# Ternary layers: a slot's last token tile between the third and the fourth product, in three slots its first one ahead of the sixth

## The chip, the cores and the metric

The kernel runs on one core of a Trainium2 chip. Its five engines run their own instruction streams and meet at semaphores: TensorE (PE; its weight loads are shown apart as PEld), VectorE (DVE), ScalarE (ACT), GpSimd (POOL) and SyncE (SP, which here issues all transfers). The metric is the time of one execution on the device in microseconds; the kernel before took 1720.47 us (median of 3 runs, 1720.34 to 1723.22).

## The reference, cut to what matters

2048 tokens of width 512 (4 x 512 tokens; every half-step works on 1024 tokens at once) go through six blocks. The change touches the two ternary feed-forward blocks alone.

```python
x = x + 0.5 * _L0_ffn_ref(_layernorm(x), W1, W2, W3)      # hidden width 2048, Hadamard transform
x = x + _L0_attn_ref(_layernorm(x), qkv, o_proj, ...)     # causal attention
x = x + 0.5 * _L0_ffn_ref(_layernorm(x), W1, W2, W3)
x = x + 0.5 * _L1_ffn_ref(_layernorm(x), gate_w, up_w, down_w, gate_s, up_s, down_s)   # ternary
x = x + _L1_attn_ref(_layernorm(x), B, C, D)              # state = tanh(x B'); state C' + D x
x = x + 0.5 * _L1_ffn_ref(_layernorm(x), gate_w, up_w, down_w, gate_s, up_s, down_s)   # ternary

def _L1_ffn_ref(x, gate_w, up_w, down_w, gate_s, up_s, down_s):   # weights are -1, 0 or 1; width 1408
    g = jnp.einsum('th,ih->ti', xf, gate_w) * gate_s
    u = jnp.einsum('th,ih->ti', xf, up_w) * up_s
    hdn = jax.nn.silu(g) * u
    out = jnp.einsum('ti,hi->th', hdn, down_w) * down_s
```

## The kernel before, in words

**Passes and slots.** A feed-forward block on 1024 tokens (a pair of 512-token chunks) is a pass. There are eight: numbers 0 to 3 are of kind "A" (hidden width 2048), and 4 to 7 of kind "B", the ternary ones, two before and two after the small state-space block. A ternary pass has 11 slots, 0 to 10. A slot computes one block of 128 hidden units, gate and up, for both chunks, and TensorE works the slots off one after the other in `run`.

**The seven products.** Gate and up times two chunks would be eight products of this size; the kernel forms seven from sums of operands. They are run as p1, p5, p6, p2 (`first_half`) and p7, p3, p4 (`second_half`). A product is 2 contraction blocks, and each of these 2 matmuls of 128x512 in a ternary pass, where the weights have no low part (4 matmuls in all): the values are split in a high and a low part, which are multiplied apart (L521, L523, L525 in `three`). Results lie in banks BX, BY, BZ, BW, BV of PSUM (0 to 4). Between the products other engines move partial sums: ScalarE copies BX to BY after p1 (`seed_y`, L1270), for which p6 waits; it copies BY to BW after p7 (`seed_w`, L1319), for which p4 waits; VectorE adds BY and the kept p5 into BZ after p6 (`seed_z`, L1956), for which p7 waits. Then come VectorE's sum L1960, its two products with the gate (`gated`, L1967 behind ScalarE's L1328, and L1971 behind p4), and the split of the hidden block in high (ScalarE, L1291) and low (VectorE, `hid_low`, L1946).

**Token tiles.** The down projection of a group of 2 or 3 finished hidden blocks is done in tiles of 128 tokens by 512 outputs, 4 matmuls (6 for the group of 3). A pass has 8 tiles for each group, four of them, here called t0 to t3, in each of the slots 3 to 9. They stand between p2 and p7. TensorE writes a tile to a bank, and VectorE adds it to y (`add_tile`, L1926 for the first group, L1929 for others). Slots 0, 1, 2 and 10 have no tiles.

**Transposes.** The next pass needs its input, normed and transposed. In four slots of each of passes 4, 5 and 6 (4 to 7, in pass 5 5 to 8), TensorE transposes two normed tiles, n0 and n1, 4 matmuls of 128x128 each (`turn_tiles`, L763), between t3 and p7; ScalarE copies them out (L1155). Pass 7 has none. In pass 5 GpSimd also multiplies these normed tiles by a row and adds them to x (L1736, L1737).

**What sets the order and the banks.** The order of instructions on each engine is written out by hand. The banks of tiles and transposes are dealt out beforehand in `Plan`: 5, 6, 7 in turn, in the order t0, t1, t2, t3, n0, n1. Before a tile or a transpose is written, `bank_free` waits for the reader of the bank's user before it: for n0 that is the add of t1, and for n1 the add of t2. On VectorE the add of t0 stands ahead of `seed_z` (`behind` in `ternary_slot`), and the other three behind it, with statistics and final adds of the pass before between them in some slots (`extra`).

**Weights.** SyncE issues the loads in order: for each slot the up and gate weights of the next one (`w13_load`, 1.8 MB in three transfers, after p4 of the slot before) and a w2 block of 512 KB (`w2_load`, L565) in one of four places, after the last tile of the group that used the place. The first group, of blocks 0 to 2, ends with slot 4's t3; block 4 goes in block 0's place, and slot 5's tiles need it.

Of the kernel before, what the change touches and what calls it, by code (L numbers as in the profile page):

```python
# [74 lines left out]
class Pass:  # L75
# [4 lines left out]
    def __init__(self, no, kind, li, pair, u0, v0, w2_0):  # L80
        self.no, self.kind, self.li, self.pair = no, kind, li, pair
        self.u0, self.v0, self.n, self.w2_0 = u0, v0, UNITS[kind], w2_0
        self.groups = GROUPS[kind]
        self.offset = 2 if no == 0 else 0

        self.open = (1, 2, self.n - 1) if kind == "B" else ()
        self.norms = NORMS.get(no, tuple(range(self.offset + 3, self.offset + 3 + PT // 2)))
        self.turn_slots = TURNS.get(no, tuple(range(self.offset + 4, self.offset + 4 + PT // 2)))
        self.downs = [[] for _ in range(self.n + 1)]
        self.turns = [[] for _ in range(self.n + 1)]  # L90
# [111 lines left out]
def build(nc, t):  # L202
# [8 lines left out]
    with ExitStack() as ctx:  # L211
# [510 lines left out]
        def _(pe):  # L722
# [58 lines left out]

            def first_half(ps, s, exact):
                u, v = ps.u0 + s, ps.v0 + s
# [28 lines left out]
                if after_ternary(ps, s):  # L812
                    pe.wait_ge(added, ended_before(ps, END_BANKS.index(BV)))
                product(ps, s, "p5", BV, True, exact, p5_done)
                pe.wait_ge(y_seeded, u + 1)
                product(ps, s, "p6", BY, False, exact, p6_done)
                product(ps, s, "p2", BX, False, exact, p2_done)

            def second_half(ps, s, exact):
                u = ps.u0 + s  # L820
                pe.wait_ge(z_seeded, u + 1)
                product(ps, s, "p7", BY, False, exact, p7_done)
                product(ps, s, "p3", BZ, False, exact, p3_done)
                pe.wait_ge(w_seeded, u + 1)
                product(ps, s, "p4", BW, False, exact, p4_done)
# [51 lines left out]
            def run(ps, exact=False):  # L877
                early = ps.no == BEFORE_T - 1
                for s in range(ps.n):
                    first_half(ps, s, exact)  # L880
                    if s == ps.n - 1:
# [4 lines left out]
                    if ps.no == BEFORE_T and s == 2:  # L886
                        pe.wait_ge(att_added, CH * TT)
                    for k, (g, i, d) in enumerate(ps.downs[s]):
                        down(ps, g, i, d, exact)
                        if early and k == 0 and s < ps.n - 1:  # L890
                            turn_tiles(ps, s)
                    if s < ps.n - 1:
                        if not early:
                            turn_tiles(ps, s)
                        second_half(ps, s, exact)
                if ps.kind == "B":
# [892 lines left out]
        def _(dve):  # L1789
# [80 lines left out]
            def sums(ps, step):  # L1870
# [10 lines left out]
                elif step == 2:  # L1881
                    dve.wait_ge(sums_ready, 4 * ps.no + 2)
                    tt(xn[:, 0:2, :], b22, t2, ALU.subtract).then_inc(sums_ready, 1)
                else:
                    tt(xn[:, 2:4, :], b21, t2, ALU.subtract).then_inc(sums_ready, 1)

# [74 lines left out]

            def gated(ps, s):
                u = ps.u0 + s
# [3 lines left out]
                nc.vector.scalar_tensor_tensor(own(u), own(u), scale, other(u), ALU.mult,  # L1967
                                               ALU.mult).then_inc(c22_read, 1)
                dve.wait_ge(c11_read, u + 1)
                dve.wait_ge(p4_done, ps.v0 + s + 1)  # L1970
# [148 lines left out]
            def ternary_slot(ps, s):  # L2119
# [19 lines left out]
                for k, (g, i, d) in enumerate(ps.downs[s]):  # L2139
                    if k or not behind:  # L2140
                        add_tile(ps, g, i, d)
# [3 lines left out]
                sum_c22(u)  # L2145
                gated(ps, s)
                if follower(ps) and s in END_SUMS:
# [328 lines left out]
```

## Time and profile before

| | |
|---|---|
| median of 3 runs | 1720.47 us (1720.34 to 1723.22) |
| profiled execution, own time | 1721.68 us |
| its span | 1719.9 us |
| PE busy | 1702.7 us, 99% |
| VectorE, ScalarE busy | 67%, 48% |
| granted TensorE clock | full in all 40 slices of the span |
| the four ternary passes with the state-space block | from 1201.25 to the end at 1719.9 us |

The profile is of one execution, and its times count from the start of its span. A matmul is shown with 0.39 us, but it overlaps the next one: what counts is the distance from one start to the next. A weight load (PEld) runs ahead of its matmul, so an idle time in front of a load need not be one of the matmuls. "[0.19 <-ACT psum L1319]" behind a row says that the engine idled 0.19 us before it and what ended that.

### The profile page before, as it was taken

The page shows a single profiled execution, that of the slowest core. Times are in us where ns is not written, and L with a number is a line of the kernel's source. Part 1 is how long each engine was busy: PE and PEld are TensorE (multiplying, and loading weights), DVE is VectorE, ACT ScalarE, POOL GpSimd, SP SyncE. Part 2 cuts the span into 40 slices and gives each one's busy share as a digit, 9 for nine tenths or more (in the row PEclk, how much of TensorE's full clock was granted, in tenths as well). Part 3 has the DMA queues.
Part 4 walks back from the last instruction along what each step waited for, and adds up shares of the span by engine and source line. Part 5 has one row for each costly group of instructions (what it writes and reads, how often), then busy time and mean ns, then how long its engine had stood idle before and what let it go on. Part 6 is the DMA issues. An engine that isn't in the chain of part 4 may idle for free.

```text
span 1719.9 us, 21451 instructions
## 1 busy us (share of the span) xinstructions
PE 1702.7 (99%) x7696; PEld 1391.1 (81%) x7696; DVE 1154.5 (67%) x1806; ACT 824.3 (48%) x1350; POOL 124.9 (7%) x184
## 2 busy tenths in 40 slices
PE   7999999999999999999999999999999999999998
PEld 5788888888888888888888888888787778787786
DVE  8977678677775555754446554457668769867866
ACT  5745544455675543434223343223556456655534
POOL 1000000000012220000000000000000144100001
PEclk9999999999999999999999999999999999999999
DMA  9775555699985000244345343344656653466666
GB/s 331 266 287 216 220 198 194 237 364 367 371 337 206 1 1 1 106 170 151 137 154 193 137 165 137 148 156 165 220 220 223 237 211 118 146 221 227 233 220 221
DMA packets 89627, 340.34 MB, mean 198 GB/s; under 512 B 9392, under 2 KB 20016, under 8 KB 83888
## 3 DMA queue, kind: packets, MB, share of 16 engines
q1 hardware_dynamic: 89520, 338.94, 53.1%
q8 instruction: 64, 1.05, 0.3%
q14 instruction: 43, 0.35, 0.1%
HBM read 259.73 MB, written 79.17 MB: 197 GB/s over the span
## 4 chain that ended last, share of the span: by engine, by line
PE 93%; DVE 4%; issue 1%; ACT 1%; DMA 1%; POOL 0%; SPq 0%; ACTq 0%; DVEq 0%
PE psum L521 34%; PE psum L523 29%; PE psum L525 26%; PE psum L763 2%; DVE xc_lo L1889 1%; DVE x L1922 1%; PE psum L732 0%; DMA w<-w_kept 0%; DVE att_lo L1863 0%; PE psum L1000 0%; DVE hid L1946 0%; DMA x<-in_w2a 0%; DVE w L1909 0%; ACT fw_hi L1128 0%; DVE psum L1956 0%
## 5 line engine op out<-in xcount | busy, mean ns | idle before, releaser
L521 PE MATMUL psum<-xc_hi,w 128*128 128x512 f32 x1544 | 609.9, 395 | 2.1 <-DVE xc_lo L1889 1.0
L523 PE MATMUL psum<-xc_lo,w 128*128 128x512 f32 x1544 | 602.3, 390 | 0.0
L525 PE MATMUL psum<-xc_hi,w 128*128 128x512 f32 x928 | 361.3, 389 | 0.0
L521 PEld LDWEIGHTS psum<-xc_hi,w 128*128 128x128 f32 x1544 | 289.8, 188 | 84.0 <-ACT psum L1270 8.1
L521 PE MATMUL psum<-w,hid 128*128 128x512 f32 x864 | 338.0, 391 | 0.6 <-DVE y L1929 0.2
L525 PE MATMUL psum<-w,hid 128*128 128x512 f32 x864 | 336.5, 390 | 0.0
L523 PEld LDWEIGHTS psum<-xc_lo,w 128*128 128x128 f32 x1544 | 290.1, 188 | 56.7
L1922 DVE TENSOR_TENSOR x<-psum,x 128x512 f32<-128x512 f32 x256 | 173.2, 688 | 149.1 <-PE psum L525 148.8
L523 PE MATMUL psum<-w,hid 128*128 128x512 f32 x544 | 211.8, 389 | 0.0
L1946 DVE TENSOR_TENSOR hid<-sg,hid 128x512 fp32r<-128x512 f32 x216 | 148.9, 699 | 93.4 <-ACT hid L1291 91.4
L525 PEld LDWEIGHTS psum<-xc_hi,w 128*128 128x128 f32 x928 | 174.2, 188 | 36.4
L521 PEld LDWEIGHTS psum<-w,hid 128*128 128x128 f32 x864 | 162.1, 188 | 39.5 <-DVE x L1922 4.5
L525 PEld LDWEIGHTS psum<-w,hid 128*128 128x128 f32 x864 | 162.2, 188 | 33.8
L1319 ACT ACTIVATE psum<-psum 128x512 f32<-128x512 f32 x108 | 62.9, 582 | 232.2 <-PE psum L525 174.3
L1291 ACT ACTIVATE hid<-sg 128x512 fp32r<-128x512 f32 x208 | 127.8, 627 | 75.6 <-DVE sg L1967 55.1
L1960 DVE TENSOR_TENSOR sg<-psum,sg 128x512 f32<-128x512 f32 x108 | 74.4, 689 | 87.9 <-ACT psum L1319 86.7
L1270 ACT ACTIVATE psum<-psum 128x512 f32<-128x512 f32 x108 | 62.9, 582 | 120.0 <-PE psum L523 58.3
L523 PEld LDWEIGHTS psum<-w,hid 128*128 128x128 f32 x544 | 102.2, 188 | 20.5
L1956 DVE TENSOR_TENSOR psum<-psum,sg 128x512 f32<-128x512 f32 x108 | 75.0, 694 | 43.5 <-PE psum L525 36.8
L1707 POOL TENSOR_SCALAR var_eps<-meanvar 128x4 f32<-128x4 f32 x24 | 6.6, 275 | 1266.7 <-DVE meanvar L1809 875.7
L1313 ACT ACTIVATE sg<-psum 128x512 f32<-128x512 f32 x64 | 38.0, 593 | 89.2 <-PE psum L525 89.2
L1150 ACT ACTIVATE xn<-x,shift,rstd 128x512 f32<-128x512 f32 x88 | 65.8, 808 | 14.1 <-POOL shift L1710 14.1
(164 smaller groups left out, 2010.0 us busy)
## 6 DMA issues: line engine op xcount, KB each, us to landing
w<-w_kept SPq DMA_DIRECT2D x186, 448.0 KB, 4.3
w<-w_kept SPq DMA_DIRECT2D x93, 896.0 KB, 6.4
w<-w_kept SPq DMA_DIRECT2D x94, 512.0 KB, 7.2
w_kept<-w SPq DMA_DIRECT2D x16, 1792.0 KB, 7.4
w_kept<-prep SPq DMA_DIRECT2D x12, 1792.0 KB, 7.6
w_kept<-w SPq DMA_DIRECT2D x16, 512.0 KB, 6.3
w_kept<-prep SPq DMA_DIRECT2D x12, 512.0 KB, 8.9
att_raw<-in_att_w SPq DMA_DIRECT2D x4, 1024.0 KB, 9.0
```

The source lines that it names most:

```text
L521: pe.matmul(out, a_hi, b_hi, start=start, stop=False, skip_group_check=onto)
L523: last = pe.matmul(out, a_hi, b_lo, start=False, stop=stop and zero == "a", skip_group_check=onto)
L525: last = pe.matmul(out, a_lo, b_hi, start=False, stop=stop, skip_group_check=onto)
L1150: return copy(out, x[:, i, :], AF.Identity, bias=shift[:, i:i + 1], scale=rstd[:, i:i + 1])
L1270: copy(bank(BY), bank(BX), AF.Copy).then_inc(y_seeded, 1)
L1291: copy(hid_of(u, c)[:, 0, :], own(u) if c else sg[:, 0, :], AF.Copy).then_inc(hid_hi_ready, 1)
L1313: copy(sg[:, 0, :], bank(BX), AF.Silu, scale=gate_scale(ps, s)).then_inc(c11_read, 1)
L1319: copy(bank(BW), bank(BY), AF.Copy).then_inc(w_seeded, 1)
L1922: tt(at_x, b, at_x, ALU.add).then_inc(added, 1)
L1946: tt(h[:, 1, :], source, h[:, 0, :], ALU.subtract).then_inc(hid_ready, 1)
L1956: tt(bank(BZ), bank(BY), own(u), ALU.add).then_inc(z_seeded, 1)
L1960: tt(own(u), bank(BY), own(u), ALU.add).then_inc(c22_ready, 1)
```

## The change

In a ternary pass `run` takes the last tile, t3, out of the slot's list and hands it to `second_half`, which puts it between p3 and p4. In slots 4, 6 and 8 (`ps.ahead`) it takes t0 out too and hands it to `first_half`, which puts it between p5 and p6. In slots with transposes these now stand directly behind t2. On VectorE, t3's add goes from ahead of the sum L1960 into `gated`, between L1967 and L1971. One sum of VectorE, step 3 of `sums`, gets a wait on the sum of step 1, since an add that stood between is gone. `Plan`, and with it every bank, is as before.

```diff
--- before.py
+++ after.py
@@ -84,6 +84,8 @@
         self.offset = 2 if no == 0 else 0
 
         self.open = (1, 2, self.n - 1) if kind == "B" else ()
+
+        self.ahead = [s for blocks in self.groups[:-1] for s in (blocks[-1] + 2,) if kind == "B" and s < self.n - 1]
         self.norms = NORMS.get(no, tuple(range(self.offset + 3, self.offset + 3 + PT // 2)))
         self.turn_slots = TURNS.get(no, tuple(range(self.offset + 4, self.offset + 4 + PT // 2)))
         self.downs = [[] for _ in range(self.n + 1)]
@@ -779,7 +781,7 @@
                                  xc_lo[:, X_OF[name], k, :], start and k == 0, k == 1, "a" if exact else None, not start)
                 last.then_inc(done, 1)
 
-            def first_half(ps, s, exact):
+            def first_half(ps, s, exact, ahead=()):
                 u, v = ps.u0 + s, ps.v0 + s
                 if ps.no == 0:
                     pe.wait_ge(w13_ready, s + 1)
@@ -812,15 +814,19 @@
                 if after_ternary(ps, s):
                     pe.wait_ge(added, ended_before(ps, END_BANKS.index(BV)))
                 product(ps, s, "p5", BV, True, exact, p5_done)
+                for tile in ahead:
+                    down(ps, *tile, exact)
                 pe.wait_ge(y_seeded, u + 1)
                 product(ps, s, "p6", BY, False, exact, p6_done)
                 product(ps, s, "p2", BX, False, exact, p2_done)
 
-            def second_half(ps, s, exact):
+            def second_half(ps, s, exact, between=()):
                 u = ps.u0 + s
                 pe.wait_ge(z_seeded, u + 1)
                 product(ps, s, "p7", BY, False, exact, p7_done)
                 product(ps, s, "p3", BZ, False, exact, p3_done)
+                for tile in between:
+                    down(ps, *tile, exact)
                 pe.wait_ge(w_seeded, u + 1)
                 product(ps, s, "p4", BW, False, exact, p4_done)
 
@@ -877,7 +883,12 @@
             def run(ps, exact=False):
                 early = ps.no == BEFORE_T - 1
                 for s in range(ps.n):
-                    first_half(ps, s, exact)
+                    tiles, ahead, between = ps.downs[s], (), ()
+                    if ps.kind == "B" and tiles:
+                        tiles, between = tiles[:-1], tiles[-1:]
+                    if s in ps.ahead:
+                        tiles, ahead = tiles[1:], tiles[:1]
+                    first_half(ps, s, exact, ahead)
                     if s == ps.n - 1:
                         second_half(ps, s, exact)
                         turn_tiles(ps, s)
@@ -885,14 +896,14 @@
                         pe.wait_ge(fw_out, 16)
                     if ps.no == BEFORE_T and s == 2:
                         pe.wait_ge(att_added, CH * TT)
-                    for k, (g, i, d) in enumerate(ps.downs[s]):
+                    for k, (g, i, d) in enumerate(tiles):
                         down(ps, g, i, d, exact)
                         if early and k == 0 and s < ps.n - 1:
                             turn_tiles(ps, s)
                     if s < ps.n - 1:
                         if not early:
                             turn_tiles(ps, s)
-                        second_half(ps, s, exact)
+                        second_half(ps, s, exact, between)
                 if ps.kind == "B":
                     fill(ps, exact)
                 for g, i, d in ps.downs[ps.n]:
@@ -1882,6 +1893,7 @@
                     dve.wait_ge(sums_ready, 4 * ps.no + 2)
                     tt(xn[:, 0:2, :], b22, t2, ALU.subtract).then_inc(sums_ready, 1)
                 else:
+                    dve.wait_ge(sums_ready, 4 * ps.no + 2)
                     tt(xn[:, 2:4, :], b21, t2, ALU.subtract).then_inc(sums_ready, 1)
 
             def convert(ps, m):
@@ -1959,13 +1971,15 @@
                 dve.wait_ge(w_seeded, u + 1)
                 tt(own(u), bank(BY), own(u), ALU.add).then_inc(c22_ready, 1)
 
-            def gated(ps, s):
+            def gated(ps, s, tile=None):
                 u = ps.u0 + s
                 scale = up_s[:, s:s + 1] if ps.kind == "B" else 1.0
                 dve.wait_ge(c12_read, u + 1)
                 dve.wait_ge(c22_ready, u + 1)
                 nc.vector.scalar_tensor_tensor(own(u), own(u), scale, other(u), ALU.mult,
                                                ALU.mult).then_inc(c22_read, 1)
+                if tile:
+                    add_tile(ps, *tile)
                 dve.wait_ge(c11_read, u + 1)
                 dve.wait_ge(p4_done, ps.v0 + s + 1)
                 nc.vector.scalar_tensor_tensor(sg[:, 0, :], bank(BW), scale, sg[:, 0, :], ALU.mult,
@@ -2137,13 +2151,13 @@
                 elif not ps.downs[s]:
                     extra(ps, s, 1)
                 for k, (g, i, d) in enumerate(ps.downs[s]):
-                    if k or not behind:
+                    if 0 < k < len(ps.downs[s]) - 1:
                         add_tile(ps, g, i, d)
                     extra(ps, s, k + 1)
                 if follower(ps) and s in LAST_SUMS:
                     sums(follower(ps), LAST_SUMS[s])
                 sum_c22(u)
-                gated(ps, s)
+                gated(ps, s, ps.downs[s][-1] if behind else None)
                 if follower(ps) and s in END_SUMS:
                     sums(follower(ps), END_SUMS[s])
                 if last:
```

In the three places below the changed kernel's lines have other numbers: L523, L525, L527, L765 are L521, L523, L525, L763 of before, and on VectorE L1941, L1958, L1968, L1972, L1979, L1985 are L1929, L1946, L1956, L1960, L1967, L1971. First TensorE in slot 5 of pass 4, around the transposes (xn). Rows with w_54,hid are tiles, rows with xc_hi or xc_lo are products. Before: the last two matmuls of t2, t3, the transposes, and the start of p7:

```order
L521 MATMUL psum<-w_54,hid 128x512
L525 MATMUL psum<-w_54,hid 128x512
L521 MATMUL psum<-w_54,hid 128x512 [waits added]
L525 MATMUL psum<-w_54,hid 128x512
L521 MATMUL psum<-w_54,hid 128x512
L525 MATMUL psum<-w_54,hid 128x512
L763 MATMUL psum<-ident,xn 128x128 [waits xn_ready,added]
L763 MATMUL psum<-ident,xn 128x128 x3
L763 MATMUL psum<-ident,xn 128x128 [waits xn_ready,added]
L763 MATMUL psum<-ident,xn 128x128 x3
L521 MATMUL psum<-xc_hi,w_53 128x512 [waits z_seeded]
```

After, from the third matmul of t2:

```order
L523 MATMUL psum<-w_54,hid 128x512
L527 MATMUL psum<-w_54,hid 128x512
L765 MATMUL psum<-ident,xn 128x128 [waits xn_ready,added]
L765 MATMUL psum<-ident,xn 128x128 x3
L765 MATMUL psum<-ident,xn 128x128 [waits xn_ready,added]
L765 MATMUL psum<-ident,xn 128x128 x3
L523 MATMUL psum<-xc_hi,w_53 128x512 [waits z_seeded]
```

t3 is gone from its place, and the transposes follow t2.

The same slot from the end of p3 to the start of the next slot's p1 (which waits for c11_read). Before:

```order
L521 MATMUL psum<-xc_hi,w_53 128x512
L523 MATMUL psum<-xc_lo,w_53 128x512
L521 MATMUL psum<-xc_hi,w_53 128x512 [waits w_seeded]
L523 MATMUL psum<-xc_lo,w_53 128x512
L521 MATMUL psum<-xc_hi,w_53 128x512
L523 MATMUL psum<-xc_lo,w_53 128x512
L521 MATMUL psum<-xc_hi,w_53 128x512 [waits c11_read,w13_in0]
```

After:

```order
L523 MATMUL psum<-xc_hi,w_53 128x512
L525 MATMUL psum<-xc_lo,w_53 128x512
L523 MATMUL psum<-w_54,hid 128x512 [waits added]
L527 MATMUL psum<-w_54,hid 128x512
L523 MATMUL psum<-w_54,hid 128x512
L527 MATMUL psum<-w_54,hid 128x512
L523 MATMUL psum<-xc_hi,w_53 128x512 [waits w_seeded]
L525 MATMUL psum<-xc_lo,w_53 128x512
L523 MATMUL psum<-xc_hi,w_53 128x512
L525 MATMUL psum<-xc_lo,w_53 128x512
L523 MATMUL psum<-xc_hi,w_53 128x512 [waits c11_read,w13_in0]
```

t3, with its wait for a free bank, stands between p3 and p4, which waits for w_seeded.

VectorE in a slot of pass 4 with tiles and without statistics (y is a tile's add, psum the seed of BZ, the first sg the sum, the next two `gated`, hid the low parts). Before:

```order
L1929 TENSOR_TENSOR y<-psum,y 128x512 [waits added,down_ready]
L1956 TENSOR_TENSOR psum<-psum,sg 128x512 [waits c12_read,p5_kept,p6_done]
L1929 TENSOR_TENSOR y<-psum,y 128x512 [waits added,down_ready] x3
L1960 TENSOR_TENSOR sg<-psum,sg 128x512 [waits w_seeded]
L1967 SCALAR_TENSOR_TENSOR sg<-sg,small 128x512 [waits c22_ready,c12_read]
L1971 SCALAR_TENSOR_TENSOR sg<-psum,small,sg 128x512 [waits p4_done,c11_read]
L1946 TENSOR_TENSOR hid<-sg,hid 128x512 [waits hid_hi_ready] x2
```

After:

```order
L1941 TENSOR_TENSOR y<-psum,y 128x512 [waits added,down_ready]
L1968 TENSOR_TENSOR psum<-psum,sg 128x512 [waits c12_read,p5_kept,p6_done]
L1941 TENSOR_TENSOR y<-psum,y 128x512 [waits added,down_ready] x2
L1972 TENSOR_TENSOR sg<-psum,sg 128x512 [waits w_seeded]
L1979 SCALAR_TENSOR_TENSOR sg<-sg,small 128x512 [waits c22_ready,c12_read]
L1941 TENSOR_TENSOR y<-psum,y 128x512 [waits added,down_ready]
L1985 SCALAR_TENSOR_TENSOR sg<-psum,small,sg 128x512 [waits p4_done,c11_read]
L1958 TENSOR_TENSOR hid<-sg,hid 128x512 [waits hid_hi_ready] x2
```

One of the three adds behind the seed went between the two rows of `gated`.

## Rows read from the trace of the kernel before

**Rows 1.** The page's first lines: busy time of each engine.
```profile
span 1719.9 us, 21451 instructions
...
PE 1702.7 (99%) x7696; PEld 1391.1 (81%) x7696; DVE 1154.5 (67%) x1806; ACT 824.3 (48%) x1350; POOL 124.9 (7%) x184
```

**Rows 2.** Waits, 1201 us to the end: in total, times, longest.
```profile
PEld psum L521 <- ACT psum L1270: 8.1, 44, 0.2
PEld psum L521 <- ACT psum L1319: 8.1, 43, 0.2
...
PEld psum L521 <- DVE psum L1956: 5.6, 16, 0.8
```

**Rows 3.** Timeline (start, length), TensorE, pass 7: starts of t0, p7, p4, p6, next t0.
```profile
1659.69 0.39 PE L521 MATMUL psum<-w,hid 128*128 128x512 f32 x1
...
1663.31 0.39 PE L521 MATMUL psum<-xc_hi,w 128*128 128x512 f32 x1
...
1665.13 0.43 PE L521 MATMUL psum<-xc_hi,w 128*128 128x512 f32 x1
...
1667.93 0.42 PE L521 MATMUL psum<-xc_hi,w 128*128 128x512 f32 x1
...
1669.79 0.39 PE L521 MATMUL psum<-w,hid 128*128 128x512 f32 x1
```

**Rows 4.** Timeline, the same slot: ScalarE's copy for p4, and p4's weight load.
```profile
1664.42 0.58 ACT L1319 ACTIVATE psum<-psum 128x512 f32<-128x512 f32 x1 [3.84 <-PE psum L523]
...
1665.05 0.19 PEld L521 LDWEIGHTS psum<-xc_hi,w 128*128 128x128 f32 x1 [0.19 <-ACT psum L1319]
```

**Rows 5.** Timeline, TensorE, pass 4 slot 5: t0, t2's last, transposes, p7.
```profile
1249.89 0.39 PE L521 MATMUL psum<-w,hid 128*128 128x512 f32 x1
...
1252.38 0.39 PE L525 MATMUL psum<-w,hid 128*128 128x512 f32 x1
...
1253.52 1.04 PE L763 MATMUL psum<-ident,xn 128*128 128x128 f32 x8
1254.31 0.47 PE L521 MATMUL psum<-xc_hi,w 128*128 128x512 f32 x1
```

**Rows 6.** Timeline, VectorE, the same slot.
```profile
1250.99 0.69 DVE L1929 TENSOR_TENSOR y<-psum,y 128x512 f32<-128x512 f32 x1 [1.24 <-PE psum L525]
1251.60 0.69 DVE L1956 TENSOR_TENSOR psum<-psum,sg 128x512 f32<-128x512 f32 x1
1252.20 1.30 DVE L1929 TENSOR_TENSOR y<-psum,y 128x512 f32<-128x512 f32 x2
```

**Rows 7.** Timeline, pass 5 slot 6: three adds, and the transposes' loads.
```profile
1379.80 1.87 DVE L1929 TENSOR_TENSOR y<-psum,y 128x512 f32<-128x512 f32 x3
...
1380.53 0.42 PEld L763 LDWEIGHTS psum<-ident,xn 128*128 128x128 f32 x4 [0.43 <-DVE y L1929]
1381.13 0.42 PEld L763 LDWEIGHTS psum<-ident,xn 128*128 128x128 f32 x4 [0.17 <-DVE y L1929]
...
1381.54 0.47 PE L521 MATMUL psum<-xc_hi,w 128*128 128x512 f32 x1
```

**Rows 8.** Timeline, pass 5 slots 5 and 6: t2's add, p7, VectorE's low parts.
```profile
1368.52 0.67 DVE L1929 TENSOR_TENSOR y<-psum,y 128x512 f32<-128x512 f32 x1
...
1369.66 0.47 PE L521 MATMUL psum<-xc_hi,w 128*128 128x512 f32 x1
...
1375.38 3.31 DVE L1946 TENSOR_TENSOR hid<-sg,hid 128x512 fp32r<-128x512 f32 x2 [0.70 <-ACT hid L1291]
```

**Rows 9.** Timeline, ScalarE, pass 4 slots 9 and 10: last seed, then L1270.
```profile
1299.21 0.59 ACT L1421 ACTIVATE psum<-y 128x512 f32<-128x512 f32 x1
1300.50 0.58 ACT L1270 ACTIVATE psum<-psum 128x512 f32<-128x512 f32 x1 [0.70 <-PE psum L523]
```

**Rows 10.** The w2 load of pass 4 slot 4, its landing, and the page's median.
```profile
1242.72 0.32 SPq L565 DMA_DIRECT2D w<-w_kept  x1
...
DMA to landing us min/median/max: 3.1/3.1/3.1
...
w<-w_kept SPq DMA_DIRECT2D x94, 512.0 KB, 7.2
```

## Prediction

> **What bounds the kernel now.** I read the page's busy line first, then the waits, then the timeline of single slots. TensorE is busy 1702.7 of 1719.9 us [rows 1], so only an idle stretch of TensorE, or work added to it, can move the time. The table of waits shows how little idle time the ternary passes have left: 43 weight loads waited 8.1 us in total for ScalarE's copy at L1319 (the copy that seeds bank BW for the fourth product, p4), and 44 waited 8.1 us for its copy at L1270 (which seeds BY for the sixth, p6); for VectorE's seeding of BZ (L1956) 16 waited 5.6 us [rows 2]. These are waits of the weight load, which runs ahead of its matmul, so they overstate the loss. The loss is read from starts of matmuls. In one slot of the last pass 16 matmuls of tiles take 1663.31 - 1659.69 = 3.62 us, that is 0.2266 us each and no loss. Then p7 and p3, 8 matmuls, take 1665.13 - 1663.31 = 1.82 us: none lost. p4, p1 and p5, 12 matmuls, take 1667.93 - 1665.13 = 2.80 us where 12 x 0.2266 is 2.72: 0.08 us is lost, all of it behind p4's wait. p6 and p2, 8 matmuls, take 1669.79 - 1667.93 = 1.86 us against 1.81: 0.05 us behind p6's wait [rows 3]. The copy for p4 lasts from 1664.42 for 0.58 us, and p4's weight load goes at 1665.05 after 0.19 us of idling [rows 4]; had it come 0.2 us earlier, nothing would be lost.
>
> **What the change removes.** 28 slots (slots 3 to 9 of four passes) get a tile between p3 and p4: at least 4 matmuls, 0.91 us, more cover for a copy that is some 0.15 us late. That wait goes: 28 x 0.08 = 2.2 us at most. 12 slots (4, 6, 8 of four passes) get a tile ahead of p6, which removes p6's wait: 12 x 0.05 = 0.6 us at most. Neither adds or removes a matmul. So the gain cannot be over 2.8 us, and it is nothing at the low end, if the loss comes back at the next wait.
>
> **What it adds: the transposes lose their cover.** A slot's tiles and transposes share banks 5 to 7 in turn, in an order fixed before: t0, t1, t2, t3, then transposes n0 and n1. So n0 needs the bank of t1, and n1 the bank of t2, read out by VectorE. The plan isn't changed, but t3 no longer stands between t2 and n0. Take slot 5 of the first ternary pass. Tiles start at 1249.89, t2's last matmul at 1252.38, the transposes at 1253.52, p7 at 1254.31, 0.79 us after them [rows 5]. VectorE starts t0's add at 1250.99, which is 0.42 us after the start of t0's last matmul (1249.89 + 3 x 0.227 = 1250.57), then seeds BZ at 1251.60, then makes the adds of t1 and t2 from 1252.20 to 1253.50 [rows 6]. t2's add cannot be earlier: 1252.38 + 0.42 = 1252.80 is its start. Today that end, 1253.50, comes before n1 wants it. After the change n0 could start at 1252.38 + 0.23 = 1252.61 and p7 at 1253.40. But n1 waits for 1253.50, and p7 stands 0.41 us behind it. The rows for such a wait exist, in slot 6 of the second ternary pass, where the adds are late today: three adds at steps of 0.60 us end at 1380.48, 1381.07 and 1381.67, the transposes' loads go at 1380.53 (0.43 us of idling) and 1381.13 (0.17 us), 0.05 us behind the first two ends [rows 7]. p7 there starts at 1381.54. So here n1 goes at 1253.55 and p7 at 1253.96: 0.55 us later than without a wait. The same holds in slots whose t0 stands ahead of p6, since n1's bank is t2's there too, and for tiles of 6 matmuls, since only the last matmul counts.
>
> There are 12 slots with transposes (four each in the first three ternary passes). Ten are as above: 10 x 0.55 = 5.5 us. The other two are slots 5 and 6 of the second ternary pass. In slot 5 VectorE has statistics between the adds: t2's add runs 1368.52 to 1369.19 and p7 starts at 1369.66 already now [rows 8]. It starts no earlier after the change, but 0.91 us of t3 still has to follow: +0.9 us. In slot 6 VectorE is held up by its pair of L1946, 3.31 us from 1375.38, beside GpSimd's work, and n1 goes at 1381.13 in either order, since slot 5's transposes, which start GpSimd's work, stay where they are. What slot 5 lost is taken back by waits that slot 6 has now, and slot 6's own t3 follows late: 0.9 us for both together, and one p4 gain and one p6 gain (0.13 us) are swallowed.
>
> **The other moves.** VectorE does one add less before its sum L1960 and one more between its two products L1967 and L1971; it idles in each slot, and t3's add starts before p4 is done, so L1971 comes no later against TensorE: nothing, with 28 x 0.05 us on either side as a bound. BZ's seed ends at 1251.60 + 0.69 = 1252.29 and p7's load, in a slot without transposes, would be wanted at about 1252.38: just in time, 0, with at most 0.1 us in each of the 6 such slots of 4-matmul tiles. In slot 9 ScalarE's last seed of a tile (1299.21) now waits for t3's add, which stands one add behind L1967 instead of ahead of it, so that it comes about 0.7 us later (an estimate, one add of 0.69 us [rows 6]), and ends beside slot 10's L1270 (1300.50) [rows 9]: 4 x 0.05 = 0.2 us, between 0 and 0.4. The wait added to VectorE's fourth sum is on a sum two steps back: 0.
>
> The last move is a transfer. The w2 block that the next group needs first is loaded into the place freed by slot 4's last tile. Its issue is at 1242.72 and it lands 3.1 us later; slot 5 wants it at 1249.89 [rows 10, 5], 7.2 us after the issue. After the change t3 ends two products (and the transposes) later: from issue to slot 5's first load there remain p4, p1, p5, p6, p2, 5 x 0.907 = 4.5 us, less 0.2 because t3's result comes that much after p4's start (0.42 - 0.23), and less 0.2 because a weight load goes ahead of its matmul: 4.1 us. 3.1 fits in 4.1. The 1.8 MB of the next up weights are issued 0.9 us behind it; behind such loads the same transfer takes 7.2 us (median [rows 10]), ahead of them I take 3.1. The Trainium skill's page "DMA: Bandwidth & Descriptors", section on queues, rings and completion order, says that each DMA engine takes one ring's descriptors in order, which speaks for the same; no row here has the two in this order.
>
> **Sum.** +5.5 + 0.9 + 0.2 - 27 x 0.08 (2.2) - 11 x 0.05 (0.5) = +3.9 us. The profiled execution took 1721.68 us, so its like would take 1725.6; it lies 1.2 us over the median of the three runs (1720.47), from which the forecast is 1724.4. A difference that this kernel's measurement tells from none is 0.2%, 3.4 us.
>
> A rule that speaks against the gain: what the row shows is p4's load at 1665.05, held 0.19 us, and matmuls 0.08 us behind afterwards [rows 3, 4]. The page "TensorE: Matmul & The Clock Gate" of the Trainium skill (section on the array's 16 sub-arrays, queue depths) says that TensorE can pull weight loads ahead of matmuls in flight. By that rule p4's load could have gone early and its wait be free, and the removal would bring nothing; the row disagrees for a load that itself waits. The time by the rule alone is that of the first rival below.
>
> **Rivals.**
> - Gains that don't come back: the 0.08 and 0.05 us are the price of any semaphore that the load meets, and are paid at the tile's or p1's wait instead. For it: part of the 0.08 is spread over p1 and p5, which also wait. Against: the tiles have waits too, and 16 of them run at 0.2266 us. Then +6.6 us, 1727.1. Chance 0.09.
> - The w2 load comes late: shared with the up weights it takes up to 7.2 us, 3.1 more than the 4.1 there are, in four slots: 3.9 + 12.4 = 16.3 us, 1736.8; from 4.1 us landing it begins to cost. Chance 0.06.
> - The transposes wait less than I say, about half, because VectorE's adds run closer behind: +1.1 us, 1721.6. Against: 1380.53 and 1381.13 sit right behind the adds' ends. Chance 0.10.
> - The other side: the transposes don't wait at all (n1 finds t2's bank read before 1253.0), and the gains stand alone: -2.6 us, 1717.9. It decides at an add that ends within 0.6 us of the start of t2's last matmul; it takes 1.1. Chance 0.06.
>
> **Chances.** The forecast holds 0.69, with 1723.4 to 1725.5 as its own range (gain terms from 0.05 to 0.08 us a slot, waits of 0.5 to 0.6 us); 0.75 of it lies above the 3.4 us. Slower: 0.52 + 0.09 + 0.06 = 0.67. No change: 0.17 + 0.10 = 0.27. Faster: 0.06. The range goes to 1721.5 below, which is the third rival, and 1727.8 above, which holds the first; the far ends of the w2 case and the gain alone are left out.
>
> **What would show it.** In the changed profile: L1319's weight-load waits down from 43 to about 15, L1270's from 44 to about 32; new waits of transposes (PEld, L765) for VectorE's adds of y, about 12 of 0.4 to 0.5 us; p7 some 0.41 us behind the second group of transposes; no wait for w2 at slot 5's first tile. It is wrong if the transposes start 0.23 us behind t2's last matmul and run through, or if slots without transposes (the whole last pass) are not some 0.1 us shorter each.

## The result, and the profile after

The change made the kernel slower: 1725.22 us (median of 9 runs, 1724.27 to 1726.53) against 1720.47 us (9 runs, 1719.78 to 1723.22). The ratio is 1.0026, 95% interval 1.0017 to 1.0034, that is 4.75 us and between 2.9 and 5.8 us. The profiled execution took 1724.76 us with a span of 1723.0 us, 3.1 us more than that of before. The runs of before came out at 1720.47 us here, at 1720.79 us beside e1 to e4 and at 1721.42 us beside e5 to e8; every difference of medians below is taken against the one beside it.

Single executions differ by a microsecond in places that the change doesn't touch. The matmuls' starts do better: from the first tile of slot 3 to the first tile behind slot 10's products, in each ternary pass, lies all that the change moves. From the timelines, one profile of each kernel, in us (two profiles of the kernel before, its own and e5's, differ by 0.43 in the sum):

| kernel | pass 4 | pass 5 | pass 6 | pass 7 | sum | against before | median against before |
|---|---|---|---|---|---|---|---|
| before | 80.97 | 82.06 | 80.89 | 77.27 | 321.19 | | |
| the change | 82.50 | 83.46 | 82.45 | 76.58 | 324.99 | +3.80 | +4.75 |
| e1, t0 ahead only | 80.63 | 81.86 | 80.64 | 76.89 | 320.02 | -1.17 | 0.0 |
| e2, t3 between only | 82.83 | 83.78 | 82.85 | 76.93 | 326.39 | +5.20 | +4.7 |
| e3, t3 not with transposes | 80.48 | 81.73 | 80.43 | 76.60 | 319.24 | -1.95 | -1.2 |
| e4, banks in issue order | 80.24 | 80.22 | 80.24 | 76.60 | 317.30 | -3.89 | -3.1 |
| e5, before again | 80.90 | 82.02 | 80.74 | 77.10 | 320.76 | -0.43 | |
| e6, before, banks shifted | 83.00 | 84.22 | 83.09 | 77.07 | 327.38 | +6.19 | +6.4 |
| e7, w2 behind up weights | 89.94 | 91.24 | 89.68 | 83.72 | 354.58 | +33.4 | +33.7 |
| e8, transposes behind p7 | 80.33 | 80.66 | 80.35 | 76.73 | 318.07 | -3.12 | -3.6 |

Pass 7, which has no transposes, got 0.69 us shorter; the other three, with four pairs each, got 1.4 to 1.6 us longer. The waits of the changed kernel from 1201 us on, to be set against [rows 2] (engine, what waited, for what: us in total, times, longest; L1281 is L1270 of before, L1330 is L1319, L765 is L763, L1938 and L1941 are L1926 and L1929):

```profile
PEld psum L765 <- DVE y L1941: 8.9, 20, 1.0
PEld psum L523 <- ACT psum L1281: 6.1, 32, 0.2
PEld psum L523 <- DVE psum L1968: 5.6, 16, 0.8
PE psum L765 <- DVE y L1941: 2.9, 11, 0.6
PEld psum L523 <- ACT psum L1330: 2.8, 15, 0.2
PEld psum L765 <- DVE y L1938: 1.2, 2, 0.6
```

Both removed waits are gone as often as they should be: 43 became 15, a difference of 28, and 44 became 32, a difference of 12. In their place stand 22 waits of transposes for VectorE's adds, 10.1 us of weight loads, where before had 3 with 0.9 us. One of them, in slot 5 of pass 4, on TensorE, on the weight loads and on VectorE, answers to [rows 5, 6]:

```profile
1253.04 0.39 PE L527 MATMUL psum<-w,hid 128*128 128x512 f32 x1
1253.59 1.27 PE L765 MATMUL psum<-ident,xn 128*128 128x128 f32 x8 [0.17 <-DVE y L1941]
1254.62 0.47 PE L523 MATMUL psum<-xc_hi,w 128*128 128x512 f32 x1
```

```profile
1253.59 0.42 PEld L765 LDWEIGHTS psum<-ident,xn 128*128 128x128 f32 x4 [0.59 <-DVE y L1941]
1254.21 0.42 PEld L765 LDWEIGHTS psum<-ident,xn 128*128 128x128 f32 x4 [0.20 <-DVE y L1941]
```

```profile
1251.65 0.69 DVE L1941 TENSOR_TENSOR y<-psum,y 128x512 f32<-128x512 f32 x1 [1.23 <-PE psum L527]
1252.26 0.69 DVE L1968 TENSOR_TENSOR psum<-psum,sg 128x512 f32<-128x512 f32 x1
1252.86 1.30 DVE L1941 TENSOR_TENSOR y<-psum,y 128x512 f32<-128x512 f32 x2
```

t2's last matmul starts at 1253.04. The adds of t1 and t2 run from 1252.86 to 1254.16; n1's load goes at 1254.21, 0.05 us behind the second, and p7 0.41 us later. From the last matmul ahead of the transposes to p7 are 1.58 us; before they were 1.02 (1254.31 less 1253.29, the start before 1253.52 by one matmul): 0.56 us lost. n0's load waits too, for t1's add, but that is not an additional loss: n1 goes when t2 is read, whether n0 was early or late.

What the change gains is seen in pass 7. TensorE in slots 7 and 8 (the starts of p7, t3, p4, then slot 8's t0, p6, t1), against [rows 3]:

```profile
1676.38 0.39 PE L523 MATMUL psum<-xc_hi,w 128*128 128x512 f32 x1
...
1678.20 0.39 PE L523 MATMUL psum<-w,hid 128*128 128x512 f32 x1
...
1679.10 0.39 PE L523 MATMUL psum<-xc_hi,w 128*128 128x512 f32 x1
...
1681.82 0.39 PE L523 MATMUL psum<-w,hid 128*128 128x512 f32 x1
...
1682.73 0.39 PE L523 MATMUL psum<-xc_hi,w 128*128 128x512 f32 x1
...
1684.54 0.39 PE L523 MATMUL psum<-w,hid 128*128 128x512 f32 x1
```

From 1676.38 to 1684.54 are 36 matmuls in 8.16 us, 0.2267 us each: nothing is lost there any more. In slots 5, 7 and 9, where no tile stands ahead of p6, its wait is still there and costs 0.045 us.

### The profile page after: what moved, and what is told of

It reads as the page before. It is cut to its first block, busy times and chain, and to the rows that moved or that the text cites. A ratio compares the mean times of both kernels' runs of the same rounds, so it can differ in the third digit from the quotient of the medians.

```text
span 1723.0 us, 21451 instructions
## 1 busy us (share of the span) xinstructions
PE 1703.6 (99%) x7696; PEld 1394.9 (81%) x7696; DVE 1153.0 (67%) x1806; ACT 824.5 (48%) x1350; POOL 125.2 (7%) x184
## 4 chain that ended last, share of the span: by engine, by line
PE 92%; DVE 5%; issue 1%; ACT 1%; DMA 0%; POOL 0%; SPq 0%; DVEq 0%; ACTq 0%
PE psum L523 34%; PE psum L525 29%; PE psum L527 26%; PE psum L765 2%; DVE xc_lo L1901 1%; DVE x L1934 1%; DVE y L1941 1%; PE psum L734 0%; DVE psum L1968 0%; DMA x<-in_w2a 0%; DVE att_lo L1874 0%; PE psum L1011 0%; DVE w L1921 0%; ACT fw_hi L1139 0%; DVE hid L1958 0%
## 5 line engine op out<-in xcount | busy, mean ns | idle before, releaser
L523 PE MATMUL psum<-xc_hi,w 128*128 128x512 f32 x1544 | 608.5, 394 | 1.8 <-DVE xc_lo L1901 1.0
L525 PE MATMUL psum<-xc_lo,w 128*128 128x512 f32 x1544 | 602.1, 390 | 0.0
L527 PE MATMUL psum<-xc_hi,w 128*128 128x512 f32 x928 | 361.6, 390 | 0.0
L523 PEld LDWEIGHTS psum<-xc_hi,w 128*128 128x128 f32 x1544 | 289.9, 188 | 76.7 <-DVE psum L1968 6.8
L523 PE MATMUL psum<-w,hid 128*128 128x512 f32 x864 | 338.0, 391 | 0.5
L527 PE MATMUL psum<-w,hid 128*128 128x512 f32 x864 | 336.7, 390 | 0.0
L525 PEld LDWEIGHTS psum<-xc_lo,w 128*128 128x128 f32 x1544 | 290.3, 188 | 57.1
L1958 DVE TENSOR_TENSOR hid<-sg,hid 128x512 fp32r<-128x512 f32 x216 | 148.5, 697 | 98.2 <-ACT hid L1302 96.1
L525 PE MATMUL psum<-w,hid 128*128 128x512 f32 x544 | 211.9, 389 | 0.0
L527 PEld LDWEIGHTS psum<-xc_hi,w 128*128 128x128 f32 x928 | 174.3, 188 | 36.4
L523 PEld LDWEIGHTS psum<-w,hid 128*128 128x128 f32 x864 | 162.2, 188 | 38.4 <-DVE x L1934 4.6
L527 PEld LDWEIGHTS psum<-w,hid 128*128 128x128 f32 x864 | 162.3, 188 | 33.9
L1330 ACT ACTIVATE psum<-psum 128x512 f32<-128x512 f32 x108 | 62.7, 581 | 211.0 <-PE psum L527 174.5
L1972 DVE TENSOR_TENSOR sg<-psum,sg 128x512 f32<-128x512 f32 x108 | 74.3, 688 | 95.2 <-ACT psum L1330 93.8
L1281 ACT ACTIVATE psum<-psum 128x512 f32<-128x512 f32 x108 | 62.7, 581 | 140.5 <-PE psum L525 79.2
L525 PEld LDWEIGHTS psum<-w,hid 128*128 128x128 f32 x544 | 102.2, 188 | 20.4
L1968 DVE TENSOR_TENSOR psum<-psum,sg 128x512 f32<-128x512 f32 x108 | 75.1, 695 | 43.9 <-PE psum L527 36.8
L1324 ACT ACTIVATE sg<-psum 128x512 f32<-128x512 f32 x64 | 38.0, 593 | 89.2 <-PE psum L527 89.2
L1291 ACT ACTIVATE sg<-psum 128x512 f32<-128x512 f32 x108 | 64.2, 595 | 17.3 <-PE psum L527 15.9
```

The costliest lines, as they stand in the source:

```text
L523: pe.matmul(out, a_hi, b_hi, start=start, stop=False, skip_group_check=onto)
L525: last = pe.matmul(out, a_hi, b_lo, start=False, stop=stop and zero == "a", skip_group_check=onto)
L527: last = pe.matmul(out, a_lo, b_hi, start=False, stop=stop, skip_group_check=onto)
L1281: copy(bank(BY), bank(BX), AF.Copy).then_inc(y_seeded, 1)
L1291: copy(own(u), bank(BV), AF.Copy).then_inc(p5_kept, 1)
L1324: copy(sg[:, 0, :], bank(BX), AF.Silu, scale=gate_scale(ps, s)).then_inc(c11_read, 1)
```

## The experiments

**e1: the ahead part alone.** `run` no longer hands out t3, and VectorE adds it where it did before; t0 stays ahead of p6 in slots 4, 6, 8.

```diff
-                    if ps.kind == "B" and tiles:
-                        tiles, between = tiles[:-1], tiles[-1:]
...
-                    if 0 < k < len(ps.downs[s]) - 1:
+                    if k:
                         add_tile(ps, g, i, d)
...
-                gated(ps, s, ps.downs[s][-1] if behind else None)
+                gated(ps, s)
```

> The change with its second part alone: t0 ahead of p6 in slots 4, 6 and 8; t3 stays ahead of the transposes, as before. My theory (the transposes lose the cover of t3, each pair in 12 slots waits 0.5 us for the add of t2; removed waits give 0.08 us at p4 and 0.05 us at p6): no wait of transposes comes back, 12 x 0.05 = 0.6 us faster than before, 1719.9. Rival (removed waits return elsewhere, at any semaphore): no change. Rival (the loss comes from VectorE's add or anything in the first half of the slot): slower by 1 us or more.

Measured: 1720.81 us (11 runs) against 1720.79 (31 runs), ratio 1.0003, 0.9994 to 1.0012. The gain of 0.6 us is inside that interval (-1.0 to +2.1 us) and cannot be told from none. The timeline shows 1.17 us less in the stretches, twice what the removed waits were worth (e5 takes that up), and its waits show 32 for the copy for p6 instead of 44, and the transposes' waits as in the kernel before, 3:

```profile
PEld psum L523 <- ACT psum L1329: 8.1, 43, 0.2
...
PEld psum L523 <- ACT psum L1280: 6.1, 32, 0.2
...
PEld psum L765 <- DVE y L1940: 0.9, 3, 0.4
```

The third reading, that the loss comes from this half, is out.

**e2: the between part alone.**

```diff
-        self.ahead = [s for blocks in self.groups[:-1] for s in (blocks[-1] + 2,) if kind == "B" and s < self.n - 1]
+        self.ahead = []
```

> The change with its first part alone: t3 between p3 and p4 in 28 slots, no tile ahead of p6. My theory: the whole loss is here, 10 x 0.5 + 0.9 + 0.2 - 27 x 0.08 = +4.0 us against before, 0.5 us more than the change itself. Rival (the loss belongs to the ahead part): no slower than before.

Measured: 1725.47 us, ratio 1.0026, 1.0016 to 1.0036, in the stretches +5.20 us. The whole loss is in this half. By the medians it is as slow as the change itself (+4.7 and +4.75), so here as in e1 t0 ahead of p6 brings nothing that can be told from none. The stretches are 1.2 us over the +4.0 that was expected; the profiled execution was the slowest of the nine (1726.49). What the profile shows too little of is the gain: pass 7 got only 0.34 us shorter, 0.05 us in each of 7 slots, not 0.08. Here p6's wait costs 0.08 us a slot and not 0.05 as before, as if 0.03 us of each removed wait had come back at the next one; e5 takes that up.

**e3: t3 moved only in slots without transposes.**

```diff
-                    if ps.kind == "B" and tiles:
+                    if ps.kind == "B" and tiles and not ps.turns[s]:
                         tiles, between = tiles[:-1], tiles[-1:]
...
-                    if 0 < k < len(ps.downs[s]) - 1:
+                    if k and (ps.turns[s] or k < len(ps.downs[s]) - 1):
                         add_tile(ps, g, i, d)
...
-                gated(ps, s, ps.downs[s][-1] if behind else None)
+                gated(ps, s, ps.downs[s][-1] if behind and not ps.turns[s] else None)
```

> The change, but in the 12 slots with transposes t3 stays where it was before, ahead of them, and so does its add; the other 16 slots and the 12 tiles ahead of p6 are as in the change. My theory: the loss is only in the slots with transposes, so what is left is gain: 16 x 0.08 + 12 x 0.05 = 1.9 us faster than before, 1718.6, 6 us faster than the change. Rival (t3 between p3 and p4 costs something by itself, through VectorE's order, the w2 load or the last seed): slower than 1720.5. Rival (gains return elsewhere): 1720.5.

Measured: 1719.64 us (11 runs), ratio 0.9992, 0.9983 to 1.0001: 1.2 us under before, which the interval doesn't quite tell from none, and 5.9 us under the change; in the stretches -1.95 us, as worked out. The loss sits in the 12 slots with transposes, and in the others t3's new place costs nothing that shows.

**e4: the banks in issue order.** Every instruction stands where the change put it. In a slot with transposes `Plan` deals n0 and n1 their banks ahead of t3.

```diff
-            for g, i in tiles[s]:
+            held = tiles[s][-1:] if kind == "B" and s < ps.n and ps.no < len(PASSES) - 1 and s in ps.turn_slots else []
+            for g, i in tiles[s][:len(tiles[s]) - len(held)]:
                 self.before[self.d] = newest.get(i)
...
                     self.turn += 1
+            for g, i in held:
+                self.before[self.d] = newest.get(i)
+                newest[i] = self.d
+                self.down(ps.downs[s], g, i, 3)
+                if i == PT - 1:
+                    for b in ps.groups[g]:
+                        self.w2_slot_free[self.w2 + b + 4] = self.d - 1
```

> The change with every instruction where it is, but the banks of a slot with transposes are dealt out in the order in which they are now issued: t0, t1, t2, n0, n1, t3. So n0 waits for t0's add, n1 for t1's, and t3 for t2's. My theory (it is the bank, read out too late, that n1 waits for): all 12 waits go, in slot 5 of pass 5 too, and the gains stand: -28 x 0.08 - 12 x 0.05 + 0.2 = 2.6 us faster than before, 1717.9, over 6 us faster than the change. Rival (the transposes wait for their input tiles or for VectorE's order, not for a bank): as slow as the change, 1725.

Measured: 1717.71 us (11 runs, 1717.23 to 1718.63), ratio 0.9982, 0.9973 to 0.9991: 3.1 us faster than before and 7.8 us faster than the change. TensorE in slot 5 of pass 4, t2's last matmul, the transposes, p7:

```profile
1253.44 0.40 PE L535 MATMUL psum<-w,hid 128*128 128x512 f32 x1
1253.68 1.04 PE L773 MATMUL psum<-ident,xn 128*128 128x128 f32 x8
1254.47 0.47 PE L531 MATMUL psum<-xc_hi,w 128*128 128x512 f32 x1
```

and VectorE's adds of t1 and t2 there:

```profile
1253.26 1.31 DVE L1949 TENSOR_TENSOR y<-psum,y 128x512 f32<-128x512 f32 x2
```

The adds stand to TensorE as in the change (t1's ends at about 1253.95, t2's at 1254.57), but p7 starts at 1254.47, before t2's add has ended, 1.03 us behind t2's last matmul. So it was a bank, and nothing else that n1 needs, that made it wait. Slots 5 and 6 of pass 5 lose their own waits as well: that pass is 1.84 us shorter than before, where passes 4 and 6 are 0.7 us shorter. These 1.1 us were waits that before had too; the expected -2.6 us left them out, the stretches have -3.89.

**e5: the kernel before, profiled again.** No edit.

> The kernel before, unchanged, profiled a second time. In the first profile p4's wait costs 0.08 us and p6's 0.045 us in every plain slot; with t0 ahead of p6 alone p4's costs 0.045, and with t3 ahead of p4 alone p6's costs 0.08. If the two sizes belong to the program (what stands ahead of the wait), this profile shows 0.08 and 0.045 again and the changed stretches of the four passes sum to 321.2 us within 0.3. If they belong to the single execution, other sizes stand here, and a sum of profiles can be off by some 0.5 us for that alone.

Measured, TensorE in pass 7, slot 5 (starts of p7, p4, p6 and the next tile), against [rows 3]:

```profile
1652.77 0.39 PE L521 MATMUL psum<-xc_hi,w 128*128 128x512 f32 x1
...
1654.59 0.42 PE L521 MATMUL psum<-xc_hi,w 128*128 128x512 f32 x1
...
1657.35 0.42 PE L521 MATMUL psum<-xc_hi,w 128*128 128x512 f32 x1
...
1659.21 0.39 PE L521 MATMUL psum<-w,hid 128*128 128x512 f32 x1
```

From p4 to p6 are 2.76 us and not 2.80, so p4's wait costs 0.045 us here, and so it does in slot 4. Slot 3 of the same profile still has 0.08 (starts of p4 and p6, 2.80 us apart):

```profile
1632.60 0.43 PE L521 MATMUL psum<-xc_hi,w 128*128 128x512 f32 x1
...
1635.40 0.41 PE L521 MATMUL psum<-xc_hi,w 128*128 128x512 f32 x1
```

So neither size belongs to the program: one wait costs 0.045 or 0.08 us, and which of them can change from slot to slot in one execution. But in e2's profile p6's wait costs 0.08 us in all 24 slots where it follows a removed wait of p4, so that the order may still have a part in it; that is not shown. The sum of the stretches is 0.43 us lower than in the first profile, just outside the 0.3 that was expected of sizes that stay. What picks the size stays open.

**e6: the kernel before with shifted banks.** No instruction moves; `Plan` passes over one bank ahead of each pair, so that n0 gets t2's bank and n1 t3's.

```diff
             elif no < len(PASSES) - 1 and s in ps.turn_slots:
+                if kind == "B":
+                    self.uses += 1
```

> The kernel before with every instruction where it is; only one bank of the round is passed over ahead of each pair of transposes in the ternary passes, so that n0 takes t2's bank and n1 takes t3's. n1 then waits for the add of the tile directly ahead of it, as in the change. My theory: the same wait of 0.51 us appears in ten slots and about 1.3 us in slots 5 and 6 of pass 5 together: +6.4 us, 1727.1, with some 20 waits of transposes for VectorE's adds of y, as in the change. Rival (the order of p3, t3, p4 is what costs): as before, 1720.7.

Measured: 1727.77 us (5 runs), ratio 1.0038, 1.0024 to 1.0052, +6.4 us; in the stretches +6.19. TensorE in slot 5 of pass 4 (last matmul of t3, n0, n1, p7), and VectorE's add of t3:

```profile
1253.31 0.39 PE L527 MATMUL psum<-w,hid 128*128 128x512 f32 x1
1253.58 0.66 PE L765 MATMUL psum<-ident,xn 128*128 128x128 f32 x4
1254.48 0.66 PE L765 MATMUL psum<-ident,xn 128*128 128x128 f32 x4 [0.25 <-DVE y L1931]
1254.89 0.47 PE L523 MATMUL psum<-xc_hi,w 128*128 128x512 f32 x1
```

```profile
1253.74 0.69 DVE L1931 TENSOR_TENSOR y<-psum,y 128x512 f32<-128x512 f32 x1 [0.21 <-PE psum L527]
```

The add ends at 1254.43, n1 goes at 1254.48, p7 at 1254.89, 1.58 us behind the last matmul, to 0.01 us as in the change. The wait can be made in the old order and, by e4, unmade in the new one: it comes from the distance between a tile and the transpose that takes its bank.

**e7: the w2 block behind the up weights.** The change, with slot 4's w2 load issued one slot later, behind the up weights of slot 6.

```diff
+                    if ps.kind == "B" and s == 5:
+                        w2_load(ps.w2_0 + 4, W2_BASE[ps.kind] + 4)
-                    if (ps.no, s) != (BEFORE_S - 1, ps.n - 1):
+                    if (ps.no, s) != (BEFORE_S - 1, ps.n - 1) and (ps.kind, s) != ("B", 4):
                         w2_load(ps.w2_0 + s, W2_BASE[ps.kind] + s)
```

> The change, but in the ternary passes the w2 block that slot 5 needs is issued behind the next up weights (after p4 of slot 4) instead of ahead of them. The change's trace has it landing 3.2 us after its issue, 1.1 us before it is wanted. Behind 1.8 MB the same transfer takes about 7 us, its issue comes 1.3 us after p4's end: slot 5's first tile should wait some 4.9 us in each of 4 passes: +19.5 us over the change, 1744.5. Rival (TensorE's next tile is covered anyway, there is slack that I don't see): under +5 us over the change.

Measured: 1755.16 us (4 runs), ratio to before 1.0192, 1.0176 to 1.0207, some 29 us over the change. In pass 4 the wait itself came as worked out. The load of pass 4, its landing, and TensorE around slot 5's first tile:

```profile
L567 SPq DMA_DIRECT2D w<-w_kept x1: 430/430/430, 1248.8 to 1248.8; - x1
...
DMA to landing us min/median/max: 6.8/6.8/6.8
```

```profile
1250.77 0.39 PE L525 MATMUL psum<-xc_lo,w 128*128 128x512 f32 x1
1255.83 0.76 PE L523 MATMUL psum<-w,hid 128*128 128x512 f32 x1 [4.67 <-DMA w<-w_kept]
1256.39 0.63 PE L527 MATMUL psum<-w,hid 128*128 128x512 f32 x1
1256.82 0.63 PE L523 MATMUL psum<-w,hid 128*128 128x512 f32 x1
```

1255.83 - 1250.77 - 0.23 = 4.83 us lost. In passes 5, 6 and 7 the load landed 7.9, 7.7 and 7.5 us after its issue, and the waits cost 5.95, 5.73 and 5.59 us: 22.1 us in all, where 19.5 were expected. But the tiles behind the wait also run at 0.43 us a matmul instead of 0.227. The busy time of the stretches before, in and behind the wait (us, busy of each engine, then the granted clock as PEclk, the DMA's share, GB/s) says why:

```profile
1251.00:1255.80 4.80, 0.16 (x1) 0.00 (x0) 0.00 (x0) 2.09 (x3) 0.00 (x0) 0.93 1.02 419
1255.80:1259.60 3.80, 3.77 (x9) 3.02 (x10) 1.30 (x2) 0.00 (x0) 0.00 (x0) 0.50 0.08 31
```

With 4.8 us of idling TensorE was granted half its clock, the 1.2 GHz level, and the 12 matmuls of t0 to t2 took 5.25 us instead of 2.72, 2.5 us more. The other passes fell to the same level, but passes 6 and 7 came back sooner, in pass 7 within these tiles:

```profile
1682.17:1685.20 3.03, 3.03 (x7) 2.46 (x8) 0.95 (x2) 0.00 (x0) 0.00 (x0) 0.50 0.03 9
1685.20:1686.40 1.20, 1.20 (x6) 0.94 (x5) 1.04 (x2) 0.00 (x0) 0.00 (x0) 1.00 0.00 0
```

There the 12 matmuls took 4.24 us, 1.5 us more. The stretches of e7 are 29.6 us longer than those of the change: 22.1 us are the waits, the other 7.5 us came behind them (2.6, 1.8, 1.5 and 1.6 in passes 4 to 7), which is what the expectation left out.

**e8: the transposes behind p7.** The change, with the pair between p7 and p3 in ternary passes, banks as in the change.

```diff
                 product(ps, s, "p7", BY, False, exact, p7_done)
+                if ps.kind == "B":
+                    turn_tiles(ps, s)
...
-                        if not early:
+                        if not early and ps.kind == "A":
                             turn_tiles(ps, s)
```

> The change, but in the ternary passes the pair of transposes stands between p7 and p3 instead of ahead of p7; banks are as in the change. t2's add then has p7, 0.9 us, as its cover. My theory: the 12 waits go as with the banks in issue order, and the time is the same as there, 1717.7 (3 us faster than before). Rival (ScalarE's copies of the transposes, now later, push its copy for p4 back by more than p3 and t3 cover): p4 waits again, 0.3 us or more in 12 slots, slower than 1721.

Measured: 1717.82 us (10 runs) against 1721.42 (14 runs), ratio 0.998, 0.997 to 0.9989, 3.6 us under before; with e4's it overlaps. TensorE in slot 5 of pass 4, p7, transposes, p3, t3, p4:

```profile
1251.95 0.39 PE L523 MATMUL psum<-xc_hi,w 128*128 128x512 f32 x1
...
1252.87 1.04 PE L765 MATMUL psum<-ident,xn 128*128 128x128 f32 x8
1253.66 0.47 PE L523 MATMUL psum<-xc_hi,w 128*128 128x512 f32 x1
...
1254.67 0.39 PE L523 MATMUL psum<-w,hid 128*128 128x512 f32 x1
...
1255.59 0.40 PE L523 MATMUL psum<-xc_hi,w 128*128 128x512 f32 x1
```

The transposes run through. The copy for p4 (L1333) runs from 1254.47 to 1255.07 behind ScalarE's copies of the transposes, and p4 starts at 1255.59 without a wait. Without t3 between, p4 would be wanted at 1254.67, ahead of the copy's end: by these rows t3 is the cover that this order needs (not run).

## Why the prediction came out right, point by point

- **The transposes lose their cover: right, and shown from both sides.** The forecast was that n1 would go 0.05 us behind t2's add and p7 0.41 us after that, 0.55 us lost in ten slots. Measured 0.56 (p7 1.58 us behind the last matmul, in the change and in e6). Ten of them make 5.6 us. e3, e4 and e8 each take them away by another edit, e6 makes them with none of the change's moves. The sign was about 12 waits of transposes, and there are 22: n0's load, which waits too at no further cost, was not counted.
- **Slots 5 and 6 of pass 5: right.** From slot 5's first tile to slot 7's the timeline has 23.95 us after the change (1366.17 to 1390.12) and 23.09 before (1365.01 to 1388.10): +0.86 us, where 0.9 less one gain of 0.08 was forecast. Slot 6's loss took up slot 5's.
- **The gains: right as a sum, less sharp as single prices.** Pass 7 has 7 waits of p4 and 3 of p6 removed, 7 x 0.08 + 3 x 0.05 = 0.71 us; it got 0.69 us shorter. But the single wait costs 0.045 or 0.08 us by turns (e5), so that the same removal is worth 0.34 us for 7 waits in e2. Rival one, gains that come back elsewhere in full, is out: 36 matmuls in a row ran without loss, and pass 7 is 0.69 us shorter. That each kernel with a part of the change has a shorter pass 7 proves less, since e5, before again, is 0.17 us shorter too.
- **The rule that spoke against the gain.** The Trainium skill's page "TensorE: Matmul & The Clock Gate" (section on the array's 16 sub-arrays, queue depths) says that TensorE can pull weight loads ahead of matmuls in flight; it doesn't say what a load does that waits for a semaphore. Read as making these waits free it was wrong here: their removal gave 0.69 us in pass 7.
- **The w2 load: right.** In the change it landed 3.2 or 3.3 us after its issue in all four passes. In pass 4 it was issued at 1246.16 and landed 3.2 us later, at 1249.4; slot 5's first tile started at 1250.54, without a wait:

```profile
L567 SPq DMA_DIRECT2D w<-w_kept x1: 320/320/320, 1246.2 to 1246.2; - x1
...
DMA to landing us min/median/max: 3.2/3.2/3.2
```

  The up weights issued 0.9 us behind it (at 1247.06) did not slow it; behind them it takes 6.8 to 7.9 us (e7).
- **The last seed in slot 9: 0.2 us were forecast, about nothing came.** It started at 1301.88, 0.54 us ahead of slot 10's copy at 1302.42, and in pass 7 slot 10's p6 lost 0.02 us more than in a plain slot.
- **The sum: right, the last tenths by luck.** +3.9 us forecast, +3.80 in the stretches. The terms give 1.54, 1.47, 1.54 and -0.66 us for passes 4 to 7, measured 1.53, 1.40, 1.56 and -0.69. But the single prices were read from the same profile that the sum is compared with; against e5, the same kernel profiled again, the change is at +4.23. The medians say +4.75 with an interval from 2.9 to 5.8 us. The 0.95 us between +3.80 and the medians is inside the interval: the profiled execution of before lay 1.2 us over its median and that of the change 0.5 us under its own, and no row shows a cause.

The version that the experiments point to is e4: the change's order with the banks in issue order, 1717.71 us, faster than both. e8 is as good.

## What to carry to other kernels

Where buffers go round in an order fixed beforehand, an instruction that is moved away takes its cover with it: the one behind it comes closer to the buffer's last reader, and the price is the reader's delay (here 0.42 us to VectorE's start, 0.69 for the add, 0.05 back, so n1 went 1.17 us behind the start of t2's last matmul) less what is left between. When the order of issue changes, deal the buffers out anew in that order; here the same move is worth -3.1 instead of +4.75 us. A removed wait of some 0.19 us of a weight load is worth only 0.05 to 0.08 us of matmuls, so look first at what a move uncovers.

## What the runs showed of the hardware that was not expected

- A weight load that is held up shortly costs TensorE 0.045 us in some slots and 0.08 us in others, in the same execution and at the same place of the slot (e5). The cause is open.
- An idle stretch of 4.8 us cost 7.3 us, since the granted clock fell to 0.50 and 12 matmuls ran at 0.43 us (e7, pass 4). Longer ones, 5.73 and 5.59 us in passes 6 and 7, cost only 1.5 us on top: the clock was back at 1.00 sooner. Why is open. TensorE's waits in the ternary passes of the change, 0.6 us at the longest, left it at 1.00.
